# A deformable convolution's sampling loop: GpSimd computes the vertical distances two chunks ahead, not one

## The reference, cut to what matters

```
om = conv3x3(x, w_off) + b_off              # 27 maps: 9 off_y, 9 off_x, 9 mask
py = off_y + row + ky - 1                   # where each of the 9 taps samples
px = off_x + col + kx - 1
sampled = bilinear(x, py, px) * sigmoid(mask)
out = einsum('bckhw,ock->bohw', sampled, w) + b
out = relu(batchnorm(out)) + x
```

## Time and profile before

| | us |
|---|---|
| median of 3 runs | 832.03 (831.27 to 839.7) |
| the profiled execution | 829.57 |
| its span, first to last instruction | 827.4 |
| PE busy in the span | 620.5 (75%) |
| DVE busy | 624.9 (76%) |
| ACT busy | 530.4 (64%) |
| POOL busy | 560.5 (68%) |

### The profile page before, as it was taken

How to read it: one execution, slowest core, us unless ns; L and a number is a source line. 1 busy time by engine, 2 the same in 40 slices (tenths; PEclk the granted TensorE clock), 3 DMA queues, 4 the chain that set the end, 5 groups by cost and what they waited for, 6 DMA issues and landing times. The chain is left out here.

```text
span 827.4 us, 31946 instructions
## 1 busy us (share of the span) xinstructions
PE 620.5 (75%) x13480; PEld 474.7 (57%) x13480; DVE 624.9 (76%) x815; ACT 530.4 (64%) x838; POOL 560.5 (68%) x441
## 2 busy tenths in 40 slices
PE   5968888888699996776766767676876688577622
PEld 1325655655336664766766756675766677576622
DVE  3469999998522126788787889888888988889845
ACT  2646777776212326778688687887878788676705
POOL 3037888883230003789898999989889997988840
PEclk9988999999799999899999999989999989978867
DMA  4000000000085119668778667666765756657202
GB/s 170 1 0 2 1 0 0 0 0 0 18 209 119 20 19 213 147 141 195 176 165 197 155 164 186 160 160 163 174 174 156 183 157 153 168 145 187 77 4 101
DMA packets 40587, 92.29 MB, mean 112 GB/s; under 512 B 21263, under 2 KB 21391, under 8 KB 40208
## 3 DMA queue, kind: packets, MB, share of 16 engines
q1 hardware_dynamic: 37314, 89.57, 43.7%
q10 hardware_dynamic: 3150, 0.88, 0.5%
HBM read 79.47 MB, written 3.28 MB: 100 GB/s over the span
## 5 line engine op out<-in xcount | busy, mean ns | idle before, releaser
L1256 PE MATMUL PS<-region 64*64 64x112 f32 (+5 forms) x11136 | 378.1, 270 | 143.6 <-ACT region L1100 87.2
L1256 PEld LDWEIGHTS PS<-region 64*64 64x64 f32 (+1 forms) x11136 | 314.6, 144 | 202.5 <-ACT region L1100 112.7
L842 DVE TENSOR_TENSOR region<-PS,region 128x1024 f32<-128x1024 f32 (+1 forms) x256 | 299.2, 1204 | 66.0 <-PE PS L1256 60.2
L557 POOL TENSOR_TENSOR region<-region 128x960 f32<-128x960 f32 x128 | 239.6, 1872 | 54.8 <-DVE region L842 54.6
L1097 ACT ACTIVATE region<-region,cst 128x1152 f32<-128x1152 f32 x128 | 159.3, 1244 | 6.0 <-DMA region<-px_scratch 5.4
L1100 ACT ACTIVATE region<-region 128x1152 f32<-128x1152 f32 x128 | 149.1, 1164 | 9.2 <-PE PS L1256 3.3
L560 POOL TENSOR_TENSOR region<-region 128x320 f32<-128x320 f32 x128 | 117.0, 914 | 10.0
L853 DVE TENSOR_REDUCE region<-region 128x32 f32<-128x736 f32 x128 | 116.3, 909 | 1.3 <-POOL region L560 1.3
L1256 PE MATMUL PS<-wg,xp 64*64 64x144 f32 x1024 | 83.7, 295 | 1.1 <-issue 1.1
L486 POOL TENSOR_TENSOR region<-region,cst 128x1024 f32<-128x1024 f32 x32 | 61.4, 1918 | 31.3 <-PE PS L1331 25.2
L709 DVE SCALAR_TENSOR_TENSOR region<-region,wr (+4 forms) x57 | 73.8, 1295 | 0.1
(11 more groups left out here) (139 smaller groups left out, 626.4 us busy)
## 6 DMA issues: line engine op xcount, KB each, us to landing
region<-px_scratch SPq DMA_DIRECT2D x256, 288.0 KB, 4.7
out<-region SPq DMA_DIRECT2D x4, 512.0 KB, 3.0
region<-xp SPq DMA_DIRECT2D x8, 140.2 KB, 3.0
region<-xp SPq DMA_DIRECT2D x8, 140.1 KB, 2.9
region<-xp SPq DMA_DIRECT2D x8, 140.0 KB, 2.9
cst<-in_consts SPq DMA_DIRECT2D x1, 1102.5 KB, 8.9
region<-xp SPq DMA_DIRECT2D x8, 132.0 KB, 2.9
region<-xp SPq DMA_DIRECT2D x8, 131.9 KB, 2.8
```

The costliest lines, as they stand in the source:

```text
L557: pool.tensor_tensor(two_rows[:, :, :, 0:NA - FOLD], two_rows[:, :, :, 0:NA - FOLD], two_rows[:, :, :, FOLD:NA], ALU.add).then_inc(half_re ...
L842: v.tensor_tensor(uu[:, 2 * u:2 * u + 2, :, lo:hi], PS[:, banks:banks + 2, 0:(hi - lo) * C].rearrange("p h (a o) -> p h o a", o=C), awf[:, ...
L1256: return nc.tensor.matmul(o, l, r, start=start, stop=stop)
```

## The change

`difference` is called for the chunk after the next. Ahead of the loop GpSimd now makes the differences of chunks 0 and 1, and at step 4s it makes that of chunk s+2 where it made that of chunk s+1. `modulate`, ACT's program and all counts that others wait for stay as they are: `ad_ready` still counts the differences in the order of the chunks.

```diff
             pool.wait_ge(py_out, done(0, 2))
             difference(0, 0, c_("jrel"), ad_ready)
+            pool.wait_ge(py_out, done(1, 2))
+            difference(0, 1, c_("jrel"), ad_ready)
             pool.wait_ge(mk_out, done(0, 2))
             pool.wait_ge(ar_ready, 1)
             modulate(0, 0, aw_ready)
...
                 s = n // SPC + 1
                 if s < PAIRS * NCH:
-                    if n % SPC == 0:
-                        difference(s // NCH, s % NCH, c_("jrel"), ad_ready)
+                    if n % SPC == 0 and s + 1 < PAIRS * NCH:
+                        difference((s + 1) // NCH, (s + 1) % NCH, c_("jrel"), ad_ready)
                     if n % SPC == 2:
                         pool.wait_ge(ar_ready, s + 1)
                         modulate(s // NCH, s % NCH, aw_ready)
```

## The result

The changed kernel takes 808.13 us (median of 4 runs, 806.62 to 812.26), the kernel before 835.7 us (4 runs, 831.27 to 839.7). The ratio is 0.968, with an interval from 0.960 to 0.975. The forecast was 791, its range 785 to 808, so the sign came out and the size did not: the time lies just above the upper end. The profiled execution took 807.16 us (span 804.9) where the sum had said 788.4, and the mean granted clock went from 0.925 to 0.942.

What follows compares the result with a forecast made beforehand. A ring of waits through ACT's wait for GpSimd's difference bounds the loop; cut, GpSimd is next. Terms -39.6 - 4.6 + 3 = -41.2 from 829.57 give 788.4, plus 2.46 for the median, rounded 791; range 785 to 808.

Steps and rivals of the forecast that it cites:

- the ring: Sampling loop: GpSimd's difference, ACT's Abs and hats, PE's taps, DVE's products and GpSimd's fold wait in a circle, 13.99 us.
- GpSimd is next, at 13.36 us: Sampling loop after the change: GpSimd's folds, difference and modulate set the pace, 13.36 us a chunk.
- The chunks from step 4 to 120, -39.6: Loop from step 4 to step 120: 29 chunks at 13.36 us, 387.4 instead of 427.06 us, so -39.6.
- The end: From step 120 to the last fold's end: no difference made there, 23.5 us instead of 28.1, so -4.6.
- the start: Loop up to step 4: late taps, not the difference, hold it up; 0 taken, -2.6 to 0 possible.
- the extra difference: Ahead of the loop GpSimd makes one difference more, 1.07 us, covered by idle time; 0 taken, 1.1 if uncovered.
- What is left of the other waits, +3 of 0 to +6: PE's issue waits before 446 us: those not covered by leads could still reach GpSimd, 0 to +6 us, +3 taken.
- late work for PE grows: Rival, stretch before 446 us: denser DMA traffic doubles issue waits from 9.7 to 19.4 us, time about 803.5; chance 0.17.
- DVE wins back 0.56 us a chunk, and its add will wait for the fold: Sampling loop: DVE at 12.8 us a chunk gains on GpSimd at 13.36, until DVE's add waits for GpSimd's fold.
- The rule against the change: GpSimd's folds: SBUF interfaces shared with VectorE could stretch them, losing 3.6 us; left out of the sum.
- The modulate: Rival, first step of a chunk: DVE waits for GpSimd's modulated weights, chunk 13.96 us, time 832; no change, chance 0.06.
- Slower: Rival, sampling loop: long issue waits add 3.33 us to each chunk hit; with 16 hit, 841 us; chance 0.04.

Runs made afterwards that it cites:

- the burst: Against the changed kernel with gathers issued singly: in five later chunks the first three pairs of position loads are held, then issued together; 805.83 us, ratio 0.970.

## Why the prediction came out as it did

**What bounds the kernel, and the ring: right.** The wait that the change takes away was 78.5 us and is 0.0 (L1132); the ring no longer sets the pace anywhere.

**GpSimd is next, at 13.36 us: right.** Fifteen intervals of 13.29 to 13.41, and 1.13 us more a chunk when each difference is made twice. Their mean is 13.37, so the allowance for spread was right.

**The chunks from step 4 to 120, -39.6: too much by the waits.** The term put 13.36 on all 29 chunks, slow ones included, "if what slowed them is covered". In the nineteen it gave -19.0 where 253.8 - 276.57 = -22.8 was said; in the nine +0.4 instead of 120.2 - 135.18 = -15.0. The mean granted clock rose as expected where the waits went, from 0.93 to 0.97 in the nineteen; in the nine it stayed at 0.94.

**The end, the start, the extra difference.** From step 116 on 37.36 us for 36.9; to step 4 27.25 for 27.25. The loop began 2.0 us later. GpSimd's idle time ahead of it is the same 28.37 us, so the extra difference does not show there, and the start of the loop differs by more than that between the kernels whose stages ahead of it are alike (310.9 to 315.9 us); I put it down to nothing.

**What is left of the other waits, +3 of 0 to +6: this is the step that failed.** It measured 15.4 us in the nine (135.62 - 120.2) and 3.8 in the nineteen. With 2.0 ahead of the loop and 0.5 at the end that is the distance from 785.4 (the sum without this term) to 807.16, but for 0.1. Two of its reasons were wrong. "PE's lead of three halves should cover part of each wait": 4.18 us at PE were 3.38 us at DVE, and in the burst DVE began its last half before the stall (554.93) just behind the end of PE's work (552.85 + 1.92), so PE had no lead left when its own wait began. And the waits were taken as given, 9.7 us that could only be hidden better. But they grew. From step 4 to 40 the kernel before has 16.8 us of issue waits, 9 times, and the changed one 31.4 us, 19 times.

That is the rival "late work for PE grows", with waits nearly doubled as it had them. Its reason, a loop traffic denser by 5%, is not the one: in that very stretch nothing is denser, 172 GB/s before and 173 after. Two things come together. The first is the cut itself: without lumps the issue waits go from 2.3 to 21.5 us when the ring is cut. The second makes them long, and is a matter of order on SP's queue. Seven gathers hold the loads of positions back for some 6.5 us, the loads catch up in a burst, and while the DMA engines are full PE sits in issue waits of up to 4.2 us. Singly issued gathers take the long waits away (14.6 us in the nine), and bursts without gathers bring them back (some 10 of the 15.7 us in the nineteen).

What an issue wait is, the DMA packets in the trace tell. In the loop 80 packets of 16 KB and of the kind "instruction" land on queue 8, one every 5.0 us on the mean in the changed kernel. All 53 issue waits of PE in the changed kernel's loop end 1.2 to 1.7 us behind the landing of one of them; a moment taken at random would lie there one time in ten.

| kernel | packet landed, us | PE went on, us | issue wait, us |
|---|---|---|---|
| changed | 383.29 | 384.55 | 3.42 |
| changed | 395.94 | 397.45 | 4.18 |
| changed | 439.93 | 441.31 | 3.37 |
| burst without gathers | 557.34 | 559.01 | 4.24 |

So PE stands until its next instructions have come. From 6 to 1 us before such a landing the DMA share was 0.98 on the mean for the seven waits of over 2 us, and 0.65 for the 27 packets behind which PE did not wait. The kernel before has 80 such packets too, but behind only 18 of them does an issue wait end, without lumps behind 7. Probably PE stood waiting for ACT's hats there while its instructions came, so that the one wait hid the other; that is inferred from these counts. The lumps cost the kernel before 8.2 us less than the changed one, which fits; that in the nineteen spread lumps cost both kernels 17 us does not, and stays open.

The rows did show the price: a chunk hit by such a wait had taken 3.33 us more than 13.36, and I put half of what such waits could cost down to a lead that no row had shown at work. DVE's lead does work once it has grown. 2.6 of the 3.8 us in the nineteen are the one interval of 16.00 us, where PE did the 112 matmuls of the far taps with an issue wait of 2.16 us among them. DVE then lacked work for 5.45 us, but GpSimd for 2.22 only; and in the run with single gathers the same matmuls cost DVE 2.10 us and GpSimd nothing (13.37). First DVE in the changed kernel, then in that run:

```profile
678.41 1.23 DVE L844 TENSOR_TENSOR region<-PS,region 128x1024 f32<-128x1024 f32 x1 [5.45 <-PE PS L1258]
```

```profile
659.55 2.48 DVE L849 TENSOR_TENSOR region<-PS,region 128x1024 f32<-128x1024 f32 x2 [2.10 <-PE PS L1263]
```

**DVE wins back 0.56 us a chunk, and its add will wait for the fold: not seen.** DVE waited 2.1 us in all at its add. With the lumps its lead hardly reached the two steps, since the waits took it away as it grew; without them DVE waited there for 3.8 us, with GpSimd made slower for 26.3.

**The rule against the change: rightly left out.** The first fold's mean went from 1872 to 1876 ns, the second's from 914 to 917, together 128 x 0.007 = 0.9 us, where the prediction's rows allowed 3.6 at most. Whether that is what the Trainium skill ("GPSIMD Engine Reference", Specifications) says of the SBUF interfaces that GpSimd shares with VectorE, no run here shows.

**The other rivals.** The modulate took nothing over: the chunks would be 13.96. "Slower" wanted 16 chunks hit by an issue wait; five of 28 took 15.8 us or more, one of them for the far taps' matmuls.

**What stays open.** Why the kernel before paid 6.4 us for seven lumps in the nine and 17 us for spread ones in the nineteen. How far the instruction packets are late because the DMA engines are full, and not for another reason: the shares above go together with it, but in every run the share and the held loads changed together. Whether another queue for the gathers would do as well as issuing them singly was not tried.

## What to carry to other kernels

When a ring is cut, stalls that stood beside its waits can come out at their full length, and ones that no row shows yet can appear. List the stalls with their lengths, and count each at what it took where it did come through, until a row shows a lead that covers it. A lead needs room to grow back: half a microsecond a chunk was too little here; with 1.1 us more the nine lost 3.5 us where they had lost 15.4. A handful of small DMAs put together on a queue that also feeds a steady stream costs through the burst behind it, microseconds after they are gone; put them one by one between the stream's loads. Here that edit was worth 1% alone, and both together bring 831.76 us to 791.5, where the change alone had reached 808.13 in another set of runs.

## What was not expected of the hardware

- PE ran dry when the DMA share had been full for a while, until a packet of instructions had landed: 1.27 us of work in 4.00 at a share of 1.03, where 0.71 gave 154.63 in 198.00. Total issue waits were 62.6 us with lumps, 38.3 without, 34.0 with loads held to two pairs, 69.7 with bursts alone.
- The price lags behind its cause: in the kernel with a lump every third chunk the DMA share was 0.25 beside the lump and 1.04 behind it, and the longest stall beside that lump ended 15 us after it.
- The length of a wait counted more than the number: from step 4 to 40, 19 issue waits of up to 2.0 us became 5.4 us at DVE, 19 of up to 4.2 us became 19.9.
